# Products that nobody reads in idle stretches of TensorE, and a re-ordered start of attention, in a kernel of a mamba block, an attention block and two layers of experts

## The reference

```python
x = x + mamba_block(layernorm(x), ...)
x = x + moe(layernorm(x), gate_w, gate_b, w1, b1, w2, b2)
x = x + attention_block(layernorm(x), ...)
x = x + moe(layernorm(x), gate_w, gate_b, w1, b1, w2, b2)
```

```python
normed = layer_norm(x, ln1_g, ln1_b)
qkv = (normed @ Wqkv + bqkv).reshape(B, S, 3, H, hd)      # H = 16 heads, hd = 8
q = q * cos + rotate_half(q) * sin
k = k * cos + rotate_half(k) * sin
scores = einsum('bhqd,bhkd->bhqk', q, k) / sqrt(hd)
attn = softmax(where(causal, -inf, scores))
x = x + einsum('bhqk,bhkd->bhqd', attn, v) @ Wo + bo
return x + gelu(layer_norm(x, ln2_g, ln2_b) @ W1 + b1) @ W2 + b2

top_k(x @ gate_w + gate_b, 2)                             # 24 experts
h = gelu(einsum('bsd,edf->besf', x, w1) + b1)             # 128 -> 512
y = einsum('besf,efd->besd', h, w2) + b2                  # 512 -> 128
out = einsum('bse,besd->bsd', combine, y)
```

## Time and profile before

| what | value |
|---|---|
| time, median of 3 runs | 825.58 us (824.08 to 826.98) |
| profiled execution, its own time | 826.58 us |
| its span in the trace | 824.7 us |
| its mean granted clock | 0.894 |
| PE busy | 652.3 us (79%) |
| DVE busy | 537.1 us (65%) |
| ACT busy | 412.4 us (50%) |
| POOL busy | 378.9 us (46%) |

### The profile page before, as it was taken

One profiled execution on the slowest core, in us unless ns is written; L12 is line 12 of the kernel. 1 busy time (PEld: TensorE's weight loads), 2 busy tenths in 40 slices (PEclk: granted clock), 3 DMA queues, 4 the chain that ended last, 5 costly groups with the idle time before them and its releaser, 6 DMA issues.

```text
span 824.7 us, 19092 instructions
## 1 busy us (share of the span) xinstructions
PE 652.3 (79%) x5342; PEld 454.9 (55%) x5342; DVE 537.1 (65%) x1522; ACT 412.4 (50%) x876; POOL 378.9 (46%) x442
## 2 busy tenths in 40 slices
PE   5946888887831999992849999999997833999990
PEld 2302323335631999991415665555655523989990
DVE  6789999976652565552897777777535552565544
ACT  3645777744310555561753655665662312655660
POOL 6305999877674445552771210000132673445550
PEclk9967999999965999997775999999998955999995
DMA  7979999910011222215273111111002111222215
GB/s 207 323 235 245 247 246 248 239 63 31 24 45 49 77 70 72 69 50 153 68 256 128 40 41 40 40 38 39 2 2 76 36 45 52 80 65 72 69 43 163
DMA packets 87529, 84.32 MB, mean 102 GB/s; under 512 B 12064, under 2 KB 76696, under 8 KB 87192
## 3 DMA queue, kind: packets, MB, share of 16 engines
q1 hardware_dynamic: 81816, 71.73, 32.6%
q0 software_dynamic: 5632, 11.58, 4.3%
HBM read 37.95 MB, written 45.33 MB: 101 GB/s over the span
## 4 chain that ended last, share of the span: by engine, by line
PE 37%; POOL 6%; DVE 4%; issue 3%; DMA 1%; ACT 1%; SPq 0%; DVEq 0%; ACTq 0%; POOLq 0%
PE bank L623 6%; PE bank L632 6%; PE bank L1899 5%; PE bank L1838 4%; POOL xrows L392 3%; PE bank L1841 3%; PE bank L1875 2%; PE bank L1868 2%; PE bank L1872 2%; PE bank L1910 1%; PE bank L1994 1%; DVE t_peak L1686 1%; PE bank L616 1%; DVE X L239 1%; POOL t_ln_rs L221 1%
## 5 line engine op out<-in xcount | busy, mean ns | idle before, releaser
L1686 DVE TENSOR_REDUCE t_peak<-bank 128x1 f32<-128x512 f32 (+2 forms) x192 | 107.2, 598 | 36.3 <-PE bank L1841 35.4
L786 POOL TENSOR_TENSOR UN<-work 128x512 f32<-128x512 f32 x64 | 81.9, 1292 | 51.3 <-DVE work L1014 51.3
L428 ACT ACTIVATE t_v_tiles<-bank,t_e_b1all 128x128 f32<-128x128 f32 x224 | 64.1, 369 | 57.9 <-PE bank L623 52.5
L428 ACT ACTIVATE m_dx_tiles<-bank,m_e_b1all 128x128 f32<-128x128 f32 x224 | 64.0, 368 | 53.1 <-PE bank L623 50.1
L400 POOL DMA_INDIRECT results<-t_A,t_e_to_row x56 | 53.8, 961 | 65.6 <-issue 30.9
L400 POOL DMA_INDIRECT results<-m_XC,m_e_to_row x56 | 53.8, 961 | 64.6 <-issue 35.0
L1014 DVE TENSOR_TENSOR_SCAN work<-bank,work 128x512 f32<-128x512 f32 x64 | 76.6, 1216 | 7.8 <-POOL UN L786 7.4
L1161 PE MATMUL bank<-UN,ident 128*128 128x512 f32 x128 | 69.9, 628 | 14.6 <-POOL UN L786 13.8
L532 DVE COPY UN<-w1all 128x512 f32 x112 | 48.1, 429 | 41.6 <-PE bank L623 30.6
L1457 POOL COPY t_tabs<-t_v_tiles 128x128 f32 (+1 forms) x16 | 5.7, 359 | 142.5 <-PE bank L1899 142.3
L632 PE MATMUL bank<-w2all,t_v_tiles 128*128 x448 | 59.8, 276 | 2.4 <-ACT t_v_tiles L428 1.8
(11 more groups left out here) (326 smaller groups left out, 1522.8 us busy)
## 6 DMA issues: line engine op xcount, KB each, us to landing
xrows<-m_nothing SPq DMA_DIRECT2D x25, 1032.0 KB, 17.8
w1all<-in_e_w SPq DMA_DIRECT2D x6, 1024.0 KB, 12.4
work<-results SPq DMA_DIRECT2D x16, 256.0 KB, 4.4
m_dx_tiles<-xrows SPq DMA_DIRECT2D x56, 64.5 KB
t_v_tiles<-xrows SPq DMA_DIRECT2D x56, 64.5 KB
...
```

The source lines that it names most:

```text
L428: ins = act.activation(e.hid[:, mp, f * P:f * P + P], core.tiles(2 + mp)[:, f, :], ACT.Gelu, bias=row(e.b1all, x)[:, f:f + 1])
L786: g.tensor_tensor(hc[:, k % 4, :], h[:, k % 2, :], c_sb[:, k % 2, :], ALU.mult).then_inc(hc_ready, 1)
L1686: v.tensor_reduce(peak[p][:, qt, a, ss[0]:ss[-1] + 1], bank[:, ACROSS[a], 0:len(ss) * w].rearrange("p (j n) -> p j n", n=w), AX_X, ALU.max ...
```

## The change

A new helper `keep_busy(pe, core, f, n, ident)` makes TensorE multiply the identity matrix by itself, repeated to 512 columns, n times into bank f. Nobody reads the bank. With the float32 identity a product is recorded as two matmuls; with the bfloat16 identity (`identb`) it is one. It is put at these places: in both experts' layers behind the spread product (6 float32 products, then, after a new wait on `core.sent`, 5 in bfloat16); in the mamba stage before the last batches' transposes (2); at the start of attention (2); ahead of unit 0's peaks (4), and one bfloat16 product behind some rounds of peaks; before the last `turn_xa` of attention (2).

The start of attention is re-ordered. V is copied out of PSUM by ScalarE (`keep_v`) without its bias, and GpSimd's `values` adds the bias to each unit. `times_cos(2)` and `times_cos(3)` stand one and two norms earlier in GpSimd's program. SyncE's queue has `load(0, 0)` and `load(1, 1)` ahead of `keep(1, 1)`. The peaks of units 0 and 1 go round three pairs of banks (`ROUNDS`) and not one; for that the rotation and a transpose use other banks. Unit 0's first three rounds are read by VectorE between the parts of batches 2 and 3, and its first round on TensorE waits for the unit's own transfer alone.

```diff
+def keep_busy(pe, core, f, n, ident=None):
+
+    x = core.ident if ident is None else ident
+    for _ in range(n):
+        pe.matmul(core.tiles(f), x[:], x[:].unsqueeze(1).to_broadcast([P, TT, P]), start=True, stop=True)
...
+        keep_busy(pe, core, 4, 6)
         pe.wait_ge(e.owner_ready, 1)
         pe.wait_ge(e.place_ready, LEAD + NB)
         pe.wait_ge(core.experts_in, 16 * 2 * (NE // LOAD_EXPERTS))
+        pe.wait_ge(core.sent, 16 * TOPK * NT * e.layer)
+        keep_busy(pe, core, 4, 5, core.identb)
...
+            keep_busy(pe, core, 3, 2)
+
             def turn_xa(b):
...
-    ROT = (7, 0)
+    ROT, UN_BANK = (7, 3), (0, 1, 2, 1)
...
+    ROUNDS = (0, 2, 4, 0, 2, 4, 0, 2, 4, 2, 4, 0)
+    read_before = lambda r: max([i + 1 for i in range(r) if ROUNDS[i] == ROUNDS[r]], default=0)
...
             keep(0, 0)
-            keep(1, 1)
             for x in range(2):
                 sp.wait_ge(part_out[x][0], 16 * PLACED)
             load(0, 0)
+            load(1, 1)
+            keep(1, 1)
             keep(2, 0)
-            load(1, 1)
             keep(3, 1)
...
             times_cos(1)
             norm_pool(g, core, ln_0, 0)
+            times_cos(2)
             norm_pool(g, core, ln_0, 1)
-            times_cos(2)
+            times_cos(3)
             norm_pool(g, core, ln_0, 2)
             norm_pool(g, core, ln_0, 3)
-            times_cos(3)
...
+            def keep_v(b):
+                act.wait_ge(v_ready, LEAD + b + 1)
+                act.activation(V[:, b * TT:b * TT + TT, :], core.tiles(6), ACT.Identity).then_inc(v_kept, 1)
...
             def times_sin(b):
-                v.wait_ge(v_ready, LEAD + b + 1)
-                v.tensor_tensor(V[:, b * TT:b * TT + TT, :], core.tiles(6),
-                                bv[:].unsqueeze(1).to_broadcast([P, TT, D]), ALU.add).then_inc(v_kept, 1)
...
+            times_sin(NB - 1)
+            take_first(NB - 2)
+            rotate(NB - 1)
+            read_peaks(0, 0, 0, pair_of(0, 0))
+            take_second(NB - 2)
+            read_peaks(0, 0, 1, pair_of(0, 1))
             take_first(NB - 1)
+            read_peaks(0, 0, 2, pair_of(0, 2))
             take_second(NB - 1)
...
+            pe.wait_ge(added[1], TT)
+            keep_busy(pe, core, 7, 2)
             turn_un(0)
...
             def prepare():
+                keep_busy(pe, core, 2, 4)
                 pe.wait_ge(unit_in[0], 64)
-                for n in range(len(PEAKS)):
-                    peaks(0, 0, n)
+                first_peaks(0, 0)
+                pe.wait_ge(qk_ready, LEAD + 2 * NB)
+                pe.wait_ge(sin_ready, LEAD + 2 * NB)
+                pe.wait_ge(v_kept, LEAD + NB)
+                for n in range(1, len(PEAKS)):
+                    first_peaks(0, n)
+                    keep_busy(pe, core, 7, 1, core.identb)
...
             hidden(1)
+            keep_busy(pe, core, 7, 2)
             turn_xa(3)
```

80 lines of the change are left out of this document (49 added, 31 removed).

## The result

The changed kernel takes 821.82 us where the kernel before takes 824.48 us beside it (medians of 17 runs each, 2.7 us apart). The ratio is 0.995, with an interval of 0.9931 to 0.997, which is 4.1 us of 825. Neither is 9.9. It was timed three more times, on three chips: 0.9925 (0.9897 to 0.9953), 0.9938 (0.9914 to 0.9961) and 0.9943 (0.9916 to 0.997), so the gain is 4 to 6 us. A single run of the kernel before lies up to 4.2 us from its median, one of the changed kernel up to 5.6.

The account below looks back on a forecast made before the run. TensorE at the lower clock after idle stretches was taken as the bound, with VectorE's reads in attention's start. Terms -5.0 - 3.0 - 1.4 - 0.4 - 0.1 = -9.9 took 826.58 to 816.7, stated as 816 us; range 811 to 822.5.

Parts of the forecast that it names:

- Start of attention: Attention's start: filler, V on ScalarE, earlier cos, SyncE's order and six banks together save 5.0 us, bounds -3.0 and -6.3.
- Step (a): Attention's start: filler and V on ScalarE; if the clock is up, batch 0's q and k come about 1.4 us earlier.
- Step (b): Attention's start, GpSimd: cos(2) and cos(3) placed earlier, so cos(3) starts at 417.7, 4.6 us before 422.25.
- Step (c): Attention's start: SyncE's order and six banks; loads before batch 1's store, unit 0's shift 4.5 us earlier, unit 1 read 5.9 earlier.
- the second rival: Start's gain goes into ScalarE, the stores and VectorE-GpSimd blocking: start only -1.5, total -6.4, 819 us; chance 0.12.
- If the clock falls in the peaks all the same: Peaks of units 0 and 1: even at the lower clock, unit 2's peaks come at 443.9 and 4.3 us are left.
- one thing against (b): Attention's start: VectorE and GpSimd block one another, 1.9 us a meeting; one more meeting costs 1 to 1.5 us.
- Last `turn_xa`: Second routing: two products before the last turn_xa keep the clock up, -3.0 us (3.5 if throughout, 1.5 if first stretch only).
- First slots: Experts' slots 0 to 3: filler raises the clock, -1.4 us in the first layer and -0.4 in the second.
- the third rival: The filler stands in the way at the lower clock: first layer +3.5 us, start -2.4, total 827 us; chance 0.05.
- Mamba filler: Mamba stage, before the last batches' transposes: two products give -0.1 us, since TensorE waits for VectorE's norm; bounds +0.7 and -0.5.
- the clock does not follow the filler: First rival: at routing and experts the clock stays low, so only the start's gain is left, about 821 us; chance 0.15.

Follow-up runs that it names:

- after_third: The changed kernel, unchanged, timed and profiled again on the third chip, against the kernel before: ratio 0.9938 (0.9914 to 0.9961).
- nine_lean_store_b: New order, V on VectorE, 9 float32 products in expert layers, two before last turn_xa, batch 1's store ahead of both loads, against the kernel before: 0.9925.
- before_again: The kernel before, unchanged, profiled a second time; no ratio given, its start of attention took 72.69 us.
- store_first: The changed kernel with the store of batch 1 ahead of both loads again, all fillers kept, against the kernel before: ratio 0.997 (0.9937 to 1.0002).
- longer_filler: The changed kernel with 14 float32 products behind the spread product instead of 6, against the kernel before: ratio 0.9887 (0.9846 to 0.9927).
- after_again: The changed kernel, unchanged, timed and profiled again on the second chip, against the kernel before: ratio 0.9925 (0.9897 to 0.9953).
- long_late: New order and banks, 14 float32 products behind the spread product, two before last turn_xa, no mamba or start fillers, against the kernel before: 1.0026 (1.0001 to 1.0051).
- order_again: The changed kernel without any filler (new order, V on ScalarE, six banks kept), second timing, against the kernel before: ratio 0.9989 (0.9971 to 1.0007).

## Why the prediction was wrong, step by step

**The sum** was -9.9 us; by the stages of the four traces it is -2.4 (start) - 3.4 (second routing) - 0.8 (first slots) + 0.2 (second slots) + 0.6 (first routing) = -5.8, and by the timed runs 4 to 6 us. The steps that failed are the start (a third to a half of its term is missing), the experts' slots, and the mamba filler. The pair of profiles is 6.9 us apart and the medians 2.7; that is scatter of single runs.

**Start of attention, forecast -5.0, measured -2.4 (-3.3 by the larger set).** Step (a) failed twice. "If the clock is up there": the two products ran at 0.50 from 390.38 to 394.16, the clock rose at 402.4, and cos(0) starts 6.69 us behind the first transposes before (394.29 to 400.98) and after (395.63 to 402.32). In after_third the clock was up for one stretch (about 394 to 397) and fell again; there it is 6.04. And ScalarE's 7.6 us of room for V's copies was a sum over the whole stretch; there is none at its head. V's first copy (402.89 to 403.49) stands ahead of the norm of batch 2, which starts 7.75 us behind the first transposes instead of 6.45 (403.38, and 400.74 before). TensorE then waits 0.73 us for batch 1's rows, cos(1) starts 12.9 us behind the first transposes where it was 11.6 before and 10.7 in my forecast, and batch 0's store is issued 18.9 us behind them instead of 17.6. With V on VectorE and the clock rising as late (nine_lean_store_b) it is 17.9, so V's copy accounts for 1.0 of the 1.3 us.

Step (b) gave 3.0 of the 4.6 us: cos(3) starts 27.92 us behind the first transposes before and 24.88 after. But it bought little, since the chain that ended last no longer runs over it (below).

Step (c) was right in its mechanism, and its price was in the second rival: the store of batch 1. Timeline of after: loads, cos(3), parts of batch 2, store of batch 1, first peaks, ScalarE's wait, unit 0's shift:

```profile
420.37 3.67 SPq L1414 DMA_DIRECT2D t_tabs<-stacks  x8
...
420.51 2.87 POOL L1447 TENSOR_TENSOR work<-t_front,t_turn_odd 128x512 f32<-128x512 f32 x2
...
422.60 1.93 DVE L1681 TENSOR_TENSOR t_A<-t_A,t_front 128x512 f32<-128x512 f32 x2
...
424.08 4.32 SPq L1405 DMA_DIRECT2D stacks<-work  x6
...
425.32 0.40 PE L1864 MATMUL bank<-t_tabs 48*128 48x512 bf16 x2
...
429.94 0.63 ACT L1561 ACTIVATE work<-work 128x512 bf16<-128x512 f32 x1 [4.75 <-DMA stacks<-work]
...
438.94 0.18 DVE L1726 SCALAR_TENSOR_TENSOR t_shift<-t_peak,t_shift 128x16 bf16<-128x16 f32 x1 [0.51 <-DVE t_shift L1723]
```

The loads go out at 420.37 and the first peaks start at 425.32: 29.7 us behind the first transposes instead of 32.8. The store of batch 1 follows at 424.08 instead of standing ahead. ScalarE, which wants to write part 0 of batch 3 over what that store reads, waits 4.75 us for its landing. Here has to be read otherwise than I did: a batch's store is six transfers, three for q and three for k (not twelve), the row at 411.89 is the store of batch 0, and that of batch 1 goes out in the trace of before from 419.22 and has landed at 424.8.

The chain that ended last (start, length, what) enters SyncE's queue at 414.5 and leaves it at 431.7:

```profile
408.53 2.50 POOL work L1447 x2
...
413.90 0.61 DVE t_front L1686
...
417.38 2.92 DMA stacks<-t_front
...
424.08 0.43 SPq L1405
...
427.94 3.79 DMA stacks<-work
...
431.82 0.64 ACT work L1561
...
432.48 0.69 DVE work L1681
...
433.17 0.73 DVE t_peak L1694 x2
...
440.61 0.54 PE bank L235
...
441.81 0.54 PE bank L235
```

It goes from cos(1) over VectorE's parts of batch 0 to batch 0's store (landed at 420.3), the eight loads and the six transfers of batch 1's store, and from the last landing (427.94 + 3.79) to ScalarE's part, VectorE's subtraction and unit 0's reads. I had the path over cos(3) and the rotation of batch 3. Batch 1's q and k are landed at 429.9 and 431.7, which on the scale of before (1.34 us less) is 428.5 and 430.4; I had put them at 424.3 and 426.5. `take_first(3)` ends at 433.2, 431.8 on that scale, where I had 428.5. These 3.3 us cover what unit 0's shift lacks: it is made at 439.12, 43.5 us behind the first transposes against 45.2, -1.7 instead of -4.5 (-2.5 on the mean of all traces of both). With the store first, the loads are late instead, and the shift came at 44.0 and 43.3 us. Store and loads share SyncE's queue, and one or the other is late.

Behind unit 0's shift the six banks give back what was missing. Unit 1's shift is made 51.8 us behind the first transposes on the mean of the four traces, 56.5 on that of the two of before: 4.7 us, between the 4.3 and the 5.9 of the forecast. What I had not priced is the turn of the loop behind it. Unit 1's shift and TensorE's transpose of unit 2's, before and after:

```profile
450.60 0.18 DVE L1696 SCALAR_TENSOR_TENSOR t_shift<-t_peak,t_shift 128x16 bf16<-128x16 f32 x1 [0.15 <-DVE t_shift L1693]
466.84 0.40 PE L1850 MATMUL bank<-identb,t_shift 128*128 128x128 bf16 x4
...
448.08 0.18 DVE L1726 SCALAR_TENSOR_TENSOR t_shift<-t_peak,t_shift 128x16 bf16<-128x16 f32 x1 [0.15 <-DVE t_shift L1723]
466.52 0.40 PE L1888 MATMUL bank<-identb,t_shift 128*128 128x128 bf16 x4
```

That is 16.2 us before (16.0 in before_again) and 18.4 after (18.3 to 18.5 in all four traces). Windows of 5.2 us behind unit 1's shift, of before (from the clock's rise on), after and store_first:

```profile
451.50:456.70 5.20, 5.20 (x82) 3.12 (x76) 3.64 (x7) 3.07 (x4) 0.00 (x0) 1.00 0.07 21
...
448.20:453.40 5.20, 5.20 (x50) 2.97 (x45) 2.36 (x5) 2.76 (x3) 0.00 (x0) 0.50 0.00 0
...
449.30:454.50 5.20, 5.20 (x86) 3.52 (x87) 3.99 (x9) 3.15 (x4) 0.00 (x0) 1.00 0.02 3
```

TensorE is busy all the time in each, with 50 matmuls at 0.50 and 82 and 86 at 1.00. Before, the clock rises at 451.4, just behind unit 1's shift. After, it rises at 453.6, as late behind the first transposes as before (58.0 us against 57.1; 56.1 to 57.7 in the other three traces), and unit 1's shift now comes 5.5 us ahead of it. In store_first and longer_filler, where the clock was back at 444.3, the same stretch takes 15.8 us. So the step "If the clock falls in the peaks all the same, ... 4.3 us are left" failed: 4.7 us were there at unit 1's shift, and 2.3 of them went into the first turns of the loop at the lower clock. Two of the bfloat16 products stand in the chain as well, 0.54 us each (the last two rows of the chain).

I had named one thing against (b), that VectorE and GpSimd block one another. VectorE's pair of L1681 took 1.93 us while cos(3) ran at 420.51, against 1.29 alone: the two engines met, and it cost 0.6 us, not the 1.9 of the meeting at 414.18. The pair at 416.84, beside cos(2), took 1.77 us. Before, the meetings had cost more: 1.9 us there and 1.0 with cos(3) (the rotation's pair at 424.02 took 2.27 us). So this rival's share turned the other way, 1.1 us for both against 2.9. The Trainium skill's page "SBUF — State Buffer", section "SBUF: two separate sides", describes a lock for the whole instruction; the trace agrees that they hold one another up, at a third of the price that I had given a meeting (0.6 of 1.9 us).

**Last `turn_xa`, forecast -3.0.** Right: the routings of after, rows that answer to the earlier trace rows, the first layer's and the second's:

```profile
206.34 0.63 PE L577 MATMUL bank<-ident,rows 128*128 128x128 f32 x4 [2.95 <-DVE rows L199]
...
260.86 0.96 POOL L399 DMA_INDIRECT xrows<-m_sz_rows,m_e_slot  x1 [0.30 <-issue]
...
628.59 0.66 PE L577 MATMUL bank<-ident,rows 128*128 128x128 f32 x4 [0.87 <-ACT t_A L1612]
...
683.08 0.96 POOL L399 DMA_INDIRECT xrows<-t_front,t_e_slot  x1 [0.30 <-issue]
```

55.5 and 55.4 us; the second has come down from 58.9. In the changed kernel this held in all four traces. It is not certain in every kernel: five of the other ten traces with the two products took 56.8 to 58.7.

**First slots, forecast -1.4 and -0.4, measured -0.8 and +0.2.** I had counted the time between spread product and rows and found that the filler fits, but not asked what comes between its end and the rows. Rows that answer to the earlier trace rows:

```profile
249.30 0.93 PE L613 MATMUL bank<-m_e_diagonal,m_e_ones 56*128 56x168 f32 x2 [3.83 <-DVE m_e_diagonal L516]
...
250.16 8.11 PE L235 MATMUL bank<-ident 128*128 128x512 f32 x12
...
263.28 2.29 PE L235 MATMUL bank<-identb 128*128 128x512 bf16 x5 [5.02 <-DMA xrows<-m_sz_rows,m_e_slot]
...
266.02 0.47 PE L626 MATMUL bank<-ident,m_dx_tiles 128*128 128x128 f32 x1 [0.45 <-DMA m_dx_tiles<-xrows]
...
272.76 0.27 PE L626 MATMUL bank<-ident,m_dx_tiles 128*128 128x128 f32 x1
...
688.04 0.47 PE L626 MATMUL bank<-ident,t_v_tiles 128*128 128x128 f32 x1 [0.27 <-DMA t_v_tiles<-xrows]
...
693.96 0.27 PE L626 MATMUL bank<-ident,t_v_tiles 128*128 128x128 f32 x1
```

The spread product came 4 us earlier than in the earlier trace rows, with 3.83 us of idle TensorE ahead of it instead of 7.80. The filler ended at 258.3, TensorE then waited 5.02 us for the sends, and the five short products ran at the lower clock (2.29 us for five; 1.24 where the clock was up). Slot 0 to slot 3: 6.74 us. Where the spread product came late (after_again, after_third: 7.4 us of idle ahead of it), there was no hole in the first layer, and it took 5.3 us: my figure of 5.2. In the second layer of the same two traces there was no hole either, and it took 5.98 and 6.48, so my term had the right size only where the clock stayed up, and I know no rule for when it does. The wait for the sends itself cost the rows nothing (slot 0 is 4.2 us behind the last send, 4.4 before). That the products would run into the rows is the third rival, and it came true in long_late alone.

**Mamba filler, forecast -0.1.** From the start of the last scan to the first transposes of the routing it is 26.9 to 27.0 us in all eight traces with it and in nine of the twelve without; the other three take 27.7 to 27.9. So it gave 0.2 us there on the mean, as forecast; VectorE is the engine waited for. What I did not see is that it seems to move the dip. Without it the clock fell within 186 to 204 in ten traces of twelve, where it costs nothing or 0.9 us. With it, it fell behind 204, in the routing, in six traces of eight, and the first routing took 57.1 us on the mean of those eight and 55.6 on that of the twelve. Windows of order_again (no filler) and of after_third, on the same chip:

```profile
186.00:204.00 18.00, 14.26 (x64) 8.68 (x63) 14.30 (x52) 6.43 (x10) 14.22 (x24) 0.91 0.15 61
204.00:212.00 8.00, 6.67 (x58) 6.06 (x56) 4.41 (x24) 2.97 (x5) 4.48 (x5) 1.00 0.01 2
```

```profile
186.00:204.00 18.00, 13.67 (x66) 8.31 (x64) 13.60 (x53) 8.28 (x12) 13.75 (x23) 1.00 0.08 36
204.00:212.00 8.00, 7.35 (x40) 7.38 (x41) 3.09 (x20) 1.11 (x2) 3.77 (x3) 0.62 0.01 2
```

1.00 and 0.62 in 204 to 212, and 55.3 against 58.5 us for the routing. That the filler causes it is inferred from the counts; no run takes it alone away.

**The rivals.** The first ("the clock does not follow the filler") holds for attention's start and for the first slots in part of the traces, not for the second routing. The second (ScalarE and the stores) is seen in the chain, together with the path over SyncE's queue that I had not. The median of 821.82 lies inside my range of 811 to 822.5, which had to hold both. The miss is in the change: 2.7 us by the medians and 4.1 by the ratio, where I gave 9.9.
